# A mixture-of-experts block on one core: the combine scatter adds into one row per token instead of writing into two

## The reference

```
xn = (x - mean) / sqrt(var + 1e-5)
attention: y = xn U; softmax(-|y_t - y_j|^2) xn, block by block
shared:    silu(xn sg) * (xn su) @ sd                    (1024 hidden columns)
routed:    each token picks its 2 best of 8 experts, with weights that sum to 1
           each expert takes the first 320 tokens that picked it, in token order
           eout   = (silu(xg rg) * (xg ru)) @ rd         (512 hidden columns)
           routed = zeros.at[token].add(weight * eout)
out = x + attention + shared + routed
```

## Time and profile before

| | us |
|---|---|
| time, median of 3 runs | 180.15 |
| the runs | 179.72, 180.15, 181.58 |
| span of the profiled execution, first to last instruction | 177.3 |
| PE busy | 168.0 |
| DVE busy | 101.1 |
| ACT busy | 95.1 |
| POOL busy | 83.1 |

### The profile page before, as it was taken

One profiled execution on the slowest core, in us unless ns is written; L12 is line 12 of the kernel. 1 busy time (PEld: TensorE's weight loads), 2 busy tenths in 40 slices (PEclk: granted clock), 3 DMA queues, 4 the chain that ended last, 5 costly groups with the idle time before them and its releaser, 6 DMA issues.

```text
span 177.3 us, 3078 instructions
## 1 busy us (share of the span) xinstructions
PE 168.0 (95%) x1075; PEld 144.2 (81%) x1075; DVE 101.1 (57%) x246; ACT 95.1 (54%) x196; POOL 83.1 (47%) x89
## 2 busy tenths in 40 slices
PE   6798999999999999999999999999999999999970
PEld 6786766896799978888678899999998999888960
DVE  3997778999743746666987543242342432415484
ACT  2349967944789055557556455664655553344100
POOL 5230420004777777778450028768677683532000
PEclk9999999999999999999999999999999999999996
DMA  5999999800111111000473006364472100101994
GB/s 166 310 196 155 267 282 334 253 6 15 63 48 59 39 51 31 5 0 0 86 247 118 0 0 183 107 220 113 142 240 71 37 18 22 37 15 32 297 284 122
DMA packets 29117, 20.72 MB, mean 117 GB/s; under 512 B 2253, under 2 KB 25832, under 8 KB 29104
## 3 DMA queue, kind: packets, MB, share of 16 engines
q1 hardware_dynamic: 27312, 17.89, 37.9%
q0 software_dynamic: 1792, 2.65, 4.7%
HBM read 12.36 MB, written 7.92 MB: 114 GB/s over the span
## 4 chain that ended last, share of the span: by engine, by line
PE 68%; DVE 10%; ACT 7%; DMA 7%; SPq 4%; issue 2%; POOLq 1%; DVEq 0%; POOL 0%
PE bank L1147 13%; PE bank L939 12%; PE bank L941 9%; PE bank L940 9%; PE bank L1015 8%; DVE yR L797 5%; PE bank L1059 4%; ACT yL L490 4%; DVE silu L791 4%; DMA row<-routed_dram 3%; SPq L325 3%; DMA sw_raw<-in_L_ffn_su_dram 3%; PE bank L988 2%; PE bank L1000 2%; PE bank L1127 2%
## 5 line engine op out<-in xcount | busy, mean ns | idle before, releaser
L482 ACT ACTIVATE silu<-bank 128x512 f32<-128x512 f32 (+1 forms) x64 | 33.1, 517 | 29.9 <-PE bank L941 29.8
L394 POOL DMA_INDIRECT slots_dram<-row,slot_i x32 | 32.6, 1018 | 27.5 <-issue 27.5
L791 DVE TENSOR_TENSOR hid_e<-bank,silu 128x320 f32<-128x320 f32 x32 | 15.7, 491 | 35.1 <-ACT silu L482 35.1
L400 POOL TENSOR_TENSOR ew_lo<-ew_raw,ew_hi 128x1024 fp32r<-128x1024 f32 x8 | 19.1, 2383 | 22.3 <-ACT ew_hi L504 22.3
L408 POOL DMA_INDIRECT routed_dram<-eo,xg x24 | 23.0, 960 | 13.1 <-ACT eo L518 7.1
L939 PE MATMUL bank<-xnT_hi,sw_hi 128*128 128x512 f32 x64 | 26.1, 408 | 0.5 <-ACT silu L482 0.5
L941 PE MATMUL bank<-xnT_hi,sw_lo 128*128 128x512 f32 x64 | 25.1, 393 | 0.0
L940 PE MATMUL bank<-xnT_lo,sw_hi 128*128 128x512 f32 x64 | 25.0, 391 | 0.0
L1147 PE MATMUL bank<-rd,hid_e 128*128 128x128 f32 (+1 forms) x192 | 23.7, 276 | 0.0
L1147 PEld LDWEIGHTS bank<-rd,hid_e 128*128 128x128 f32 (+1 forms) x192 | 22.0, 173 | 1.0
L939 PE MATMUL bank<-xgT_hi,ew_hi 128*128 128x320 f32 x64 | 21.1, 330 | 0.0
(11 more groups left out here) (146 smaller groups left out, 264.9 us busy)
## 6 DMA issues: line engine op xcount, KB each, us to landing
ew_raw<-in_L_ffn_rg_dram SPq DMA_DIRECT2D x8, 256.0 KB, 2.9
ew_raw<-in_L_ffn_ru_dram SPq DMA_DIRECT2D x8, 256.0 KB, 3.1
rd<-in_L_ffn_rd_dram SPq DMA_DIRECT2D x8, 256.0 KB, 2.9
routed_dram<-fill SPq DMA_DIRECT2D x1, 2048.0 KB, 12.4
row<-routed_dram SPq DMA_DIRECT2D x8, 256.0 KB, 4.7
slots_dram<-fill SPq DMA_DIRECT2D x1, 1300.0 KB, 13.2
xg<-slots_dram SPq DMA_DIRECT2D x8, 130.0 KB, 2.9
acc<-in_L_attn_x_dram SPq DMA_DIRECT2D x4, 256.0 KB, 4.0
```

Of the source, the lines that this page charges most:

```text
L394: G.indirect_dma_start(slots_dram, bass.IndirectOffsetOnAxis(slot_i[:, k, t:t + 1], 0), row[:, t, 0:RW], None, bounds_check=E * CAP - 1, o ...
L400: G.tensor_tensor(ew_lo[:, e % 2, :, :], ew_raw[:, e % 2, :, :], ew_hi[:, e % 2, :, :].bitcast(F32), ALU.subtract).then_inc(ew_ready, 1)
L482: C.activation(silu[:, q % 2, 0:n], gate_b[q % 2][:, 0:n], ACT.Silu).then_inc(silu_ready, 1)
L791: V.tensor_tensor(hid, up_b[q % 2][:, 0:n], silu[:, q % 2, 0:n], ALU.mult).then_inc(hid_ready, 1)
```

## The change

`routed_dram` becomes T + 1 rows. Both choices of a token aim at the same row, its token number; the filler row of an unused slot is row T. The scatter gets a compute operation, add, and its bounds check now raises an error at an index beyond T, where before a filler's index 2T was skipped. Since two experts can now aim at one row, and the addition reads the row before it writes it, `write_routed(e)` waits on POOL until the three scatters of expert e - 1 have landed. The zero fill covers T rows and, in a second transfer, row T. The end reloads one tensor: four transfers of 256 KB instead of eight, and one addition of 128x512 per block instead of two.

```diff
-    routed_dram = nc.dram_tensor("routed_dram", (2 * T, D), F32).ap()
+    routed_dram = nc.dram_tensor("routed_dram", (T + 1, D), F32).ap()
...
-    routed_v = routed_dram.rearrange("(k b t p) d -> k b p t d", k=2, b=B, p=P)
+    routed_v = routed_dram[0:T, :].rearrange("(b t p) d -> b p t d", b=B, p=P)
...
-        routed = [row1[:, :, 2:RW], row2[:, :, 2:RW]]
+        routed = row1[:, :, 2:RW]
...
-            sp.dma_start(routed_dram.rearrange("(p a) d -> p a d", p=P),
-                         fill[:, 2:RW].rearrange("p (o d) -> p o d", o=1).to_broadcast([P, 2 * T // P, D])
+            sp.dma_start(routed_dram[0:T, :].rearrange("(p a) d -> p a d", p=P),
+                         fill[:, 2:RW].rearrange("p (o d) -> p o d", o=1).to_broadcast([P, T // P, D])
                          ).then_inc(routed_zeroed, 16)
+            sp.dma_start(routed_dram[T:T + 1, :], fill[0:1, 2:RW]).then_inc(routed_zeroed, 16)
...
             for g in range(B):
-                for k in range(2):
-                    sp.dma_start(routed[k][:, TG * g:TG * g + TG, :], routed_v[k, g]
-                                 ).then_inc(routed_loaded[g], 16)
+                sp.dma_start(routed[:, TG * g:TG * g + TG, :], routed_v[g]).then_inc(routed_loaded[g], 16)
...
-            G.iota(fill[:, 1:2].bitcast(I32), pattern=[[0, 1]], base=2 * T, channel_multiplier=0
+            G.iota(fill[:, 1:2].bitcast(I32), pattern=[[0, 1]], base=T, channel_multiplier=0
...
-            G.iota(row2[:, :, 1].bitcast(I32), pattern=[[P, NT]], base=T, channel_multiplier=1)
+            G.iota(row2[:, :, 1].bitcast(I32), pattern=[[P, NT]], base=0, channel_multiplier=1)
...
                 pool.wait_ge(eo_ready, e + 1)
+                if e > 0:
+                    pool.wait_ge(eo_written[(e - 1) % 2], 48 * ((e - 1) // 2 + 1))
                 for r in range(3):
                     n = P if r < 2 else TAIL
                     G.indirect_dma_start(
                         routed_dram, bass.IndirectOffsetOnAxis(xg[0:n, e % XB, r, 1:2].bitcast(I32), 0),
                         eo[0:n, e % 2, r, :], None,
-                        bounds_check=2 * T - 1, oob_is_err=False).then_inc(eo_written[e % 2], 16)
+                        bounds_check=T, oob_is_err=True, compute_op=ALU.add).then_inc(eo_written[e % 2], 16)
...
-            pool.wait_ge(routed_zeroed, 16)
+            pool.wait_ge(routed_zeroed, 32)
...
-                dve.wait_ge(routed_loaded[g], 32)
+                dve.wait_ge(routed_loaded[g], 16)
                 ts = slice(TG * g, TG * g + TG)
-                then(V.tensor_tensor(acc[:, ts, :], routed[0][:, ts, :], acc[:, ts, :], ALU.add))
-                V.tensor_tensor(acc[:, ts, :], routed[1][:, ts, :], acc[:, ts, :], ALU.add
-                                ).then_inc(summed, 1)
+                V.tensor_tensor(acc[:, ts, :], routed[:, ts, :], acc[:, ts, :], ALU.add).then_inc(summed, 1)
```

## The result

The changed kernel takes 183.87 us in the median of 4 runs (183.43 to 184.15), the kernel before 179.96. The ratio is 1.019, with an interval of 1.014 to 1.025. Forecast was 177.4. Both kernels were measured side by side twice more, with 1.020 (1.013 to 1.028) and 1.022 (1.018 to 1.025).

What follows compares the result with a forecast made beforehand. PE bounds the kernel almost throughout, the routed path with its byte-bound reload the end. Profiled 177.3 less 2.95 plus 0.2 gives 174.55; for the median, 180.15 less 2.75 gives 177.4 us, range 176.8 to 181.7.

Steps and rivals of the forecast that it cites:

- The scatter adds: Last expert's scatters and expert stage: the add costs 1.3 us at the end, 1.1 hidden behind PE, 0.2 paid.
- The added wait: POOL's wait before each expert's scatters: typical landing 1.2 us early, slowest 0.4 late, so it costs nothing.
- x: What the add adds between the start of the last expert's scatters and their landing: 1.3 us, bounds 0 and 5.9.
- What bounds the kernel before, and what the saved reload is worth: End of the program: routed path late, reload bound by bytes; halving reload and additions gains 2.95 us, then PE is late.
- The issue of an adding scatter: POOL's three issues for the last expert: doubled work per row adds 0.3 us in all.
- rival 2: Expert stage: longer issues make POOL the bound; 181.7 us at 0.6 more per issue, 188.4 at 0.97; chance 0.14.
- d: Added time for each of POOL's three scatter issues per expert; decides from 0.42 us, whole change breaks even at 0.51.
- rival 1: Tail: the read before the write is dear, landing grows several us; 179.1 us at a landing of about 5; chance 0.19.
- The landing: Landing of the scatters: putting a read in front of the write adds about 1.0 us.
- The read in front of the write: Within the scatter's landing: about 1.0 us, from a small load's 3.0 against a small store's 1.9; with 2, 178.4 in all.

Runs made afterwards that it cites:

- DVE's split: Changed kernel with the expert weights' low parts computed on DVE instead of POOL, both halves behind chunk 1: 1.014; measured again 185.56, 1.034.

## Why the prediction was wrong

The forecast said 2.75 faster; the kernel is 3.9 slower. Two steps failed, *The scatter adds* and *The added wait*. On the routed path the prediction had 4.0 saved by the reload and the additions, 1.3 lost to the adding scatter (x) and nothing to the wait. The runs show 4.6 saved, 4.8 lost to the add alone and 3.8 more with the wait: 4.0 lost in all. By these numbers the change without its wait would come out about even; that kernel wasn't run, since two experts' additions into one row would then not be ordered.

- *What bounds the kernel before, and what the saved reload is worth*: right. Half the reload with plain scatters gives 2.95 in the trace, and PE is what is late next. The four reloads of the changed kernel land 6.3 after their first issue, where about 7 was forecast.
- *The issue of an adding scatter*: wrong. I took 0.3 for three issues, by reading 1 ns per row off the 64-row and the 128-row scatter and doubling it. The doubling of the row part was right: 1.43 and 1.55 are 0.12 apart, where 0.91 and 0.97 were 0.06. What grew as well is the part that doesn't depend on rows, from 0.85 (0.97 less twice 0.06) to 1.31. I had argued that the issue is almost all fixed and that therefore it wouldn't grow; no row supported that step. The growth is 0.56 for each issue in the mean (1.517 less 0.960), 1.7 for three, and rival 2's own threshold (0.42 for PE, 0.51 for break-even) was passed.
- *Rival 2's price*: at d = 0.56 its formula gives 181.0, 2.9 below the 183.9 measured; what it lacks above all is the wait. Its period is right: 7.15 + 3 x 0.56 - 1.07 = 7.76, and the add alone shows 7.70 to 7.75. The longer split (2.9 instead of 2.37) doesn't lengthen it, since it begins about 0.47 before the third issue's record ends. But PE was 2.9 late where the formula gives 2.2. I had read PE's slack of 0.84 at expert 3; before the last expert, whose products come sooner, it is only 0.32, from the end of the split at 143.50 to the first product. Both rows are of the kernel before:

```profile
141.13 2.37 POOL L400 TENSOR_TENSOR ew_lo<-ew_raw,ew_hi 128x1024 fp32r<-128x1024 f32 x1 [1.07 <-ACT ew_hi L504]
```

```profile
143.82 0.30 PE L939 MATMUL bank<-xgT_hi,ew_hi 128*128 128x320 f32 x1
```

- *The added wait*: wrong in the step that called it free. I compared the 4.5 between the last issue of one group and the first of the next with a landing of 3.3, on the old issue lengths. With the longer issues that gap is 4.0 (154.60 to 158.61 with the add alone), the landings beside weight loads are 3.6 to 3.8 in the changed kernel, and after a landing another 0.8 pass before the next first issue. Counted round the loop of three issues, landing and release it takes 3.8 + 3.0 + 0.8 = 7.6, against a period of 7.15: it binds even with POOL otherwise free, as the kernel with DVE's split shows. Added to plain scatters the wait is free, added to adding ones it goes with 3.8, of which 1.6 are the long last landing. My rival 1 let landings matter to the expert stage only beyond 5.6; they do at 3.6 beside the split, and at 3 without it.
- *The landing*: 1.0 more was forecast. Away from the weight loads a group's last scatter shows 2.9 to 3.0 against 2.1, so 0.8 to 0.9. But the last group of the changed kernel took 4.19, 4.07 and 4.07 in its three profiles, and 4.51 with add, wait and the old reload; with the add alone it took 2.95, with DVE's split 3.0 to 3.2. Why is open; 1.1 to 1.2 of the changed kernel's tail hang on it. So x, forecast as 1.3, is 2.0 with the add alone and 3.2 in the changed kernel.
- *The read in front of the write*: beside the Trainium skill ("DMA: Bandwidth & Descriptors", section "Latency and other measured facts"), which has 0.2 us for an average DRAM access and 2 at high load, the 0.8 lies between, in windows in which the DMA share is 0.4.
- *DVE's four additions, the zero fill, the iotas, the bounds check*: as forecast, none of them shows in the time; only the check was measured by itself.

## What to carry to other kernels

An added wait must be counted round its whole loop, with the lengths that the other edits of the same change give it: issue, landing, release, next issue, against the period of the stage. Of two edits one can be free alone (the wait) and the other cost 4.8 (the add), and together they cost 8.6. A slack read at one expert isn't that of the last one. Where a transfer gets a new operation, its issue on the engine that prepares it can be a cost of its own beside its landing, here 0.56 for each. And where a transfer at the end is bound by bytes, look first for fewer bytes by the same plain transfers, if the result may be rounded.

## What the runs showed of the hardware that was not expected

- An indirect scatter of 128 rows of 512 B with an add occupies POOL for 1.55 instead of 0.97, and a group's last one lands in 2.9 to 3.0 instead of 2.1 when no weights are loaded (the last group of some kernels apart, as said above). Beside weight loads it is 3.6 to 3.8 in the changed kernel and 3.9 to 4.5 with DVE's split; before, 3.3 and 3.9 are seen there as well as 2.1.
- The add also makes the DMA engines busier for the same bytes. In the 3 us from the start of a group's third scatter, with no other traffic to speak of, the share is 0.11 before (from 152.78) and 0.39 after (from 159.66), both at 33 GB/s. The page's row of GpSimd's queue (packets, MB, share of the 16 engines' span), which also holds the dispatch scatters, before and after; with the add alone it has the same 3968 packets:

```profile
q0 software_dynamic: 1792, 2.65, 4.7%
```

```profile
q0 software_dynamic: 3968, 2.65, 10.4%
```

- The next compute instruction on POOL starts 0.96 after the start of the last adding scatter, while that is still shown as running, and takes 2.9 instead of 2.37.
- On some chips every kernel measured, the one before included, took some 33 us more. The traces taken there show it in the attention stage: from 50 to 90 us PE is busy for 9 to 12 us where it is busy for 39.6 on the other chips, with DVE and ACT nearly idle too (2 to 3 us and 5 to 6 us busy, against 24 and 23) while POOL's dispatch scatters go on. PE's granted clock, 1.00 in the first 50 us, is 0.50 to 0.56 from 60 to 70 us, in which PE is busy for 0 to 3 us; 0.50 is the lower level, 1.2 GHz. What caused the idle time wasn't investigated.
